# A decoder layer with routed experts: the first routing set spread over earlier steps, two normalisations moved to ScalarE, and fp16 slot marks

## The reference

```python
def attn(x):                                  # "pooling" attention along the sequence
    h = layer_norm(x, gamma, beta)
    keys, values = h @ Wk.T + bk, h @ Wv.T + bv
    w = exp((keys @ Wka.T + bka) / 16)
    w = w / cumsum(w, axis=1)
    return cumsum(w * keys, axis=1) * values
def xattn(q, ctx, mask): ...                  # 16 heads, softmax over the 77 context rows, then @ W_o.T
def ffn(x):
    top_v, top_i = top_k(x @ router_w.T + router_b, 2)
    top_w = softmax(top_v)
    out = sum over e of (gelu(x @ w1[e].T + b1[e]) @ w2[e].T + b2[e]) * weight of e in top_w
    return layer_norm(out + x, ln_w, ln_b)
x = layernorm(x + attn(x))                    # x1 in the kernel
x = layernorm(x + xattn(x, ctx, mask))        # x2
x = layernorm(x + ffn(x))
```

## Time and profile before

| | us |
|---|---|
| median of 3 runs (lowest, highest) | 539.31 (537.64, 541.08) |
| profiled execution, its time | 541.87 |
| profiled execution, span of the core | 540.1 |
| PE busy (share of the span) | 501.5 (93%) |
| DVE busy | 374.5 (69%) |
| ACT busy | 251.0 (46%) |
| POOL busy | 260.0 (48%) |
| 16 DMA engines, mean rate | 173 GB/s |

### The profile page before, as it was taken

The page is one execution under the profiler, slowest core; times in us unless marked ns, Lnnn a source line. Parts: engine busy times, 40 slices in busy tenths (PEclk is TensorE's granted clock), DMA queues, the critical chain, the costliest instruction groups (busy, mean ns, idle before and its releaser), DMA issues.

```text
span 540.1 us, 10882 instructions
## 1 busy us (share of the span) xinstructions
PE 501.5 (93%) x3286; PEld 450.1 (83%) x3286; DVE 374.5 (69%) x1114; ACT 251.0 (46%) x835; POOL 260.0 (48%) x369
## 2 busy tenths in 40 slices
PE   6789999989999869988999999999999999999991
PEld 5657888878888757878799999999999999999980
DVE  3767979858677886537977667665667656766774
ACT  3436666756666436653244334344443334444320
POOL 4534222212212240418267666665676756766565
PEclk9879999999999979999999999999999999999997
DMA  8109930835575625406546666666666665666420
GB/s 231 12 4 302 348 113 6 273 112 180 176 234 172 198 74 210 152 21 229 183 127 214 220 225 206 202 192 194 211 220 227 217 208 202 203 215 231 143 51 1
DMA packets 57280, 93.69 MB, mean 173 GB/s; under 512 B 12018, under 2 KB 49017, under 8 KB 52103
## 3 DMA queue, kind: packets, MB, share of 16 engines
...
q10 hardware_dynamic: 1632, 0.27, 0.3%
...
## 4 chain that ended last, share of the span: by engine, by line
PE 35%; issue 19%; POOL 19%; DVE 16%; DMA 7%; ACT 2%; POOLq 1%; ACTq 0%; SPq 0%; DVEq 0%
PE psum_b L1495 8%; PE psum_v L1628 6%; PE psum_a L1594 6%; DMA work<-weighed_outputs,routing 4%; POOL routing L772 4%; POOL out L776 4%; POOL work L768 3%; POOL work L763 3%; PE psum_m L1646 2%; POOL front_then_w_ring L729 2%; DMA weighed_outputs<-work 2%; PE psum_m L1495 2%; DVE routing L1364 2%; PE psum_c L1615 2%; PE psum_a L1739 1%
## 5 line engine op out<-in xcount | busy, mean ns | idle before, releaser
L969 ACT ACTIVATE front_then_w_ring<-psum_a,front_then_w_ring 128x128 f32<-128x128 f32 x160 | 45.8, 369 | 73.3 <-PE psum_a L1739 73.3
L879 ACT ACTIVATE work<-psum_a,score_max 128x77 f32<-128x77 f32 x256 | 62.4, 335 | 34.4 <-DVE score_max L1136 34.3
L1739 PEld LDWEIGHTS psum_a<-front_then_w_ring 128*128 128x128 f32 x640 | 74.4, 192 | 3.9 <-issue 3.0
L1739 PE MATMUL psum_a<-front_then_w_ring 128*128 128x128 f32 x640 | 75.1, 275 | 2.6 <-ACT front_then_w_ring L959 2.0
L969 ACT ACTIVATE front_then_w_ring<-psum_b,front_then_w_ring 128x128 f32<-128x128 f32 x152 | 43.3, 369 | 69.1 <-PE psum_b L1739 69.1
L1762 PE MATMUL psum_v<-expert_w,front_then_w_ring 128*128 x320 | 72.7, 380 | 0.1
L1739 PEld LDWEIGHTS psum_b<-front_then_w_ring 128*128 128x128 f32 x608 | 70.9, 192 | 0.9
L1739 PE MATMUL psum_b<-front_then_w_ring 128*128 128x128 f32 x608 | 71.1, 275 | 0.0
L1762 PE MATMUL psum_c<-expert_w,front_then_w_ring 128*128 x304 | 68.8, 379 | 0.0
L1762 PEld LDWEIGHTS psum_v<-expert_w,front_then_w_ring 128*128 128x128 f32 x320 | 59.3, 190 | 7.6 <-issue 0.4
L1762 PEld LDWEIGHTS psum_c<-expert_w,front_then_w_ring 128*128 128x128 f32 x304 | 56.3, 190 | 6.9
...
## 6 DMA issues: line engine op xcount, KB each, us to landing
...
```

The costliest lines, as they stand in the source:

```text
L879: last = act.activation(prob[:, u % RING_U, at_k:at_k + SC], pa[:, H % 2, g * SC:(g + 1) * SC], ACT.Exp, bias=smax[:, j % 2, head:head + 1])
L969: last = act.activation(hidT[t % 2][:, c, :], src[:, n, q * P:(q + 1) * P], ACT.Gelu, bias=bias[:, c:c + 1])
L1739: last = pe.matmul(dst[:, n, q * P:(q + 1) * P], w1[:, k, c * P:(c + 1) * P], xtT[t % 2][:, k, :], start=(k == 0), stop=(k == KD - 1))
```

## The change

1. *Sets.* `FIRST` is 7, and the sets have 7 and 9 tiles: 14 and 18 pairs. `RANKS_STEP` is one higher (50). The choice of the first set is cut into `first_top` (step 41), `first_hot` (44) and `second_choice` (47); counts, ranks and the start of `first_map` are at 50, the map and a part of the placing (`place_later`) at 51, the rest at 52.
2. *Marks.* `cols` is fp16; a set's pairs are marked in four groups with one semaphore step a group, at steps 53 to 56 for the first set. The products wait for a group at a time. PE's `mark_pairs(0)` is at step 56 as before.
3. *Norms.* `x1_normalise` of pieces 3 to 8 and `x2_normalise` of tiles 0 to 13 go from DVE to ACT, as scale and bias of one instruction a tile. POOL makes the bias: two more small operations for each.
4. *Stages.* The last stages of a piece come sooner: for pieces 6 to 8 `attention` by one step, `add` and `x1` by two, `x1_turn` and `queries` by one; of pieces 3 to 5 some by one or two.
5. *Slot tiles.* Tile 0 is turned at step 61 and tile 1 at step 63 of the attention loop, and copied by ACT at 62 and behind the loop; `up(0, 0)` is PE's first work behind the loop. POOL loads tiles 0 to 3 at steps 58, 60 and 62. The ranks of the second set stand behind `up(2)`, its marks on PE before `up(5)`, on DVE in four groups between the rounds of tiles 0 to 2; the second table is read behind DVE's round of tile 3.

The core of the diff:

```diff
-FIRST = 8
+FIRST = 7
-SETS = ((0, TILES // 2), (TILES // 2, TILES // 2))
+SETS = ((0, FIRST), (FIRST, TILES - FIRST))
+MARK_GROUPS = tuple(tuple((c * n + a, c * n + b) for c in range(TOPK) for a, b in ((0, (n + 1) // 2), ((n + 1) // 2, n))) for _, n in SETS)
-RANKS_STEP = (CHUNKS - 1) * STEPS + 1
+RANKS_STEP = (CHUNKS - 1) * STEPS + 2
-                   "invert1": 10, "values": 10, "pool": 9, "times": 8, "attention": 8, "add": 6, "x1": 5, "x1_turn": 5, "queries": 4}
+                   "invert1": 10, "values": 10, "pool": 9, "times": 8, "attention": 9, "add": 8, "x1": 7, "x1_turn": 6, "queries": 5}
-        cols = tmp(P)
+        cols = tmp(P, dt=F16)
...
+                pool.tensor_scalar(x2_drop[:, j:j + 1], x2_mv[:, j, 0:1], -1.0, None, ALU.mult).then_inc(x2_drop_made, 1)
+                pool.tensor_tensor(x2_rstd[:, j:j + 1], x2_veps[:, j:j + 1], mhalf[:, 0:1], ALU.pow).then_inc(x2_pow, 1)
+                pool.tensor_tensor(x2_shift[:, j:j + 1], x2_drop[:, j:j + 1], x2_rstd[:, j:j + 1], ALU.mult).then_inc(x2_rstd_ready, 1)
...
+            def x1_normalise(p):
+                act.wait_ge(LN2["rstd_ready"], p - BY_ACT + 1)
+                for j in range(tiles_of(p)):
+                    last = act.activation(x1_of(p)[:, j, :], x_of(p)[:, j, :], ACT.Identity, scale=LN2["rstd"][:, p % 2, j:j + 1],
+                                          bias=LN2["shift"][:, p % 2, j:j + 1])
+                last.then_inc(x1_ready, 1)
...
-                if H == (CHUNKS - 1) * STEPS - 3:
-                    first_choice(0)
-                if H == (CHUNKS - 1) * STEPS - 2:
+                if H == RANKS_STEP - 9:
+                    first_top(0)
+                if H == RANKS_STEP - 6:
+                    first_hot(0)
+                if H == RANKS_STEP - 3:
                     second_choice(0)
                 if H == RANKS_STEP:
                     first_map()
+                if H == RANKS_STEP + 1:
+                    map_of(tbend, spare, FIRST, 0.0)
+                    place_later()
+                if H == RANKS_STEP + 2:
                     place(0)
...
+                if H == CHUNKS * STEPS - 3:
+                    turn_rows(0)
+                if H == CHUNKS * STEPS - 1:
+                    turn_rows(1)
```

269 lines of the change are left out of this document (162 added, 107 removed).

## The result

| | before | after |
|---|---|---|
| median of 20 runs each (lowest, highest), us | 538.75 (537.08, 542.17) | 537.14 (534.40, 541.27) |
| profiled execution, its time, us | 541.87 | 537.01 |
| profiled execution, span, us | 540.1 | 535.2 |
| PE / DVE / ACT / POOL busy, us | 501.5 / 374.5 / 251.0 / 260.0 | 496.5 / 367.2 / 261.7 / 268.9 |

The ratio is 0.9958, 95% interval 0.9939 to 0.9978: 2.3 us less (1.2 to 3.3). A second measurement of both kernels gave 0.9992 (0.9956 to 1.0027), which includes no difference at all. The forecast was 6.7 us less. The time of 537 lies in the range given, but the gain is a third of the forecast one or less.

The account below looks back on a forecast made before the run. PE bounds the attention and expert loops; the gain lies between them. Routing +7.5 and transition -0.8 give 6.7 us less: span 540.1 to 533.4, time 532.6 us after the median's 2.6 offset from the profiled time; range 525.5 to 538.5.

Parts of the forecast that it names:

- the transition: From attention loop to expert loop: 6.1 us of old waits go, new waits of 1.7, 3.1 and 2.1 come, net -0.8.
- the norms up to tile 9: x1 and x2 normalised on ACT, up to 176 us: PE's work covers all of it, 0, bounds -3 and +1.
- Routing spread: Steps 41 to 58: the 4.5 us wait and slow clock go, +9.9, less three small waits of 2.4: +7.5 us.
- (a): Step 47: last piece's sum and moments, moved to step 46, delay maximum 47; wait 0.6 us, bounds 0 and 0.9.
- (b): Step 48: ACT normalises the last piece between two sets of exponentials; wait 0.5 us, bounds 0 and 1.2.
- (c): Step 53: DVE does a residual and four mark pairs before maximum 54; wait 1.3 us, bounds 0.6 and 1.8.
- Rival 4: The 4.5 us wait merely moves to steps 50 to 56; gain 2 to 3 us, time 537; chance 0.06.
- Rival 3: Slower: ACT's x1 normalise delays exponentials in pieces 6 to 8, with low clock, 3.1 us a piece: 541.9; chance 0.07.
- (d): Behind the attention loop: PE waits for the second set's ranks from DVE; 1.7 us, bounds 1.0 and 2.9.
- (e): Early expert loop: PE reaches the second set's marks after 18.4 us, DVE needs 21.8; wait taken as 3.1 us.
- Rival 2: Long waits for marks and ranks are each followed by the lower clock; some 4 us lost, 536.6; chance 0.27.
- (f): Early expert loop: PE waits for tile 7's rows, which hang on the second table; 2.1 us, bounds 0 and 3.

Follow-up runs that it names:

- c_after: The changed kernel, unchanged, profiled and measured once more; ratio to the kernel before 0.9992 (0.9956 to 1.0027).
- b_split: Kernel before with only the first set's map and placing cut from one block into three, behind the maxima of steps 49 to 51; ratio 0.9952.
- n_x1: Changed kernel with the normalisation of x1 alone back on DVE (piece 3's one step later), x2's left on ACT; ratio to before 0.9966.
- m_early: Changed kernel with the second set's last mark group ahead of DVE's tile 2 round, table behind it, tiles 7 to 9 loaded one round sooner; ratio 0.9889.

## Why the prediction was wrong, step by step

The measured sum, in stretches without chance (slow clock near 120 us left out): tiles 0 to 3 lose 1.3, 3 to 6 gain 0.4, 6 to 9 lose 0.2, 9 to 13 gain 7.4 to 8.0, 13 to `down(10)` lose 3.6 to 6.0. That is a gain of 0.3 to 3.3 us, about the two measured ratios (0.4 and 2.3). Against the forecast of 6.7 that is 3.4 to 6.4 us too little. Most of it failed in one step, the transition: forecast -0.8, measured -3.6 to -6.0. There the wait for the marks was 5.1 and not 3.1, and the slow clock behind it, which the sum put at nothing, cost 2.0 to 2.4. The other failed step is the norms up to tile 9, forecast 0: with the stages these three stretches lost 1.1.

1. *Routing spread, +7.5.* The size was right (7.4 to 8.0, no wait above 1.1 us; the loop's end at 222.1, of which 3.2 us are the early start, and at 224.6 in c_after), and the three small waits came near their sizes: 0.7 for (a) and 0.3 for (b) against 0.6 and 0.5, 1.1 for (c) against 1.3; 0.5 for the turning of the last piece (L1613) was not foreseen. The reason was not: "the 4.5 us wait has no cause left" took one block for a cause that the earlier choice and the norms shared. That the size came out is partly luck: the stretch holds (each by the run that undoes it) 2.0 us of norms and 0.6 of marks, which the forecast put at nothing here, and a loss of 1.6 by the moved stages. Rival 4 (the wait merely moves, time 537) has the right time by luck: its mechanism is what the block alone does (b_split), not the whole change.
2. *Norms, 0 with bounds of -3 and +1.* This step failed, though within its bounds. "Up to 176 us PE covers all of it" looked at DVE, which gets relief, and not at ACT, where 1.2 us stand ahead of exponentials that PE needs: 1.2 us lost in tiles 0 to 3 (n_x1). Behind tile 9 the same edit is worth 2.0. Rival 3 had this mechanism, but for pieces 6 to 8, where all that showed was (b)'s 0.3.
3. *Stages.* I gave them nothing of their own; they cost 1.75.
4. *Marks, 0.42 a pair.* A pair alone took 0.385: the estimate of 0.39 by the Trainium skill's table ("VectorE: DVE Perf Modes", "The perf-mode tier table (the rule you actually need)") was right. The saving of 0.07 a pair that I had from the slope of the fp32 rows gives the same 0.39; only the middle that I took between it and no saving was off. But eighteen pairs took 9.2 us and not 7.6: two places were held beside POOL's work.
5. *(d) Ranks, 1.7.* Measured 1.8. DVE took 3.2 us for the choice (239.27 to 242.51), and no operation was held.
6. *(e) Marks, 3.1.* Measured 5.1. My own terms give 3.4 (21.8 - 18.4), and I took 3.1. From the ranks to the last mark DVE took 24.0 us and not 21.8: 1.6 for the marks, 0.6 for rounds of 11.0 instead of 10.4.
7. *The clock.* Rival 2, to which I gave 0.27, is what happened, for one of its two waits: 2.4 us behind (e) (2.0 in c_after, `up(5)` 5.78 us), and none behind (d) in either trace of the changed kernel. The lower clock came at (e) in each of the ten traces that keep this order of marks. It should have been in the sum and not in a rival: the kernel before shows the lower clock at its one wait of that size, 4.5 us.
8. *(f) Tile 7, 2.1.* 0.2, and 0.6 in c_after (with tile 8's 0.9), since (e) and the clock had delayed PE: what is late is one chain, and 3.1 + 2.1 were two readings of its end. m_early shows it from the other side: with (e) gone, the wait for tile 7 is 2.8.
9. *Tile 0.* "Turning at step 61 finds them there" took a median of 3.6 us for the landing. PE waited 0.7 to 1.6 us in ten of the twelve traces with this order; in c_after the rows were issued at 211.96 and there at 220.88:

```profile
220.88 0.44 PE L1757 MATMUL psum_b<-identity,front_then_w_ring 128*128 128x128 f32 x2 [1.63 <-DMA front_then_w_ring<-token_rows,routing]
```

The trace of the kernel before already had this. Its list of DMA issues, narrowed to tile 0's (issued at 220.37 us), says 8.2 us where the median of all 39 is 3.6; tile 1's took 6.9. There the turning at 232 hid it.

```profile
front_then_w_ring<-token_rows,routing POOLq DMA_INDIRECT x1, 8.2
```

For the changed kernel itself the transition adds up: with the prediction's 6.1 us gone, 1.8 + 5.1 + 2.4 + 0.2 = 9.5 come, 3.4 lost, and the stretch says 3.6. In c_after 1.6 + 1.8 + 5.1 + 2.0 + 0.9 = 11.4 come, 5.3 lost, and the stretch says 6.0. I had -0.8.
